# Short key tile as one strip, and the last peaks, count, constants and value copies moved behind the pieces

## The reference, cut to what matters

```python
q = x @ Wq
xc = jnp.concatenate((mem, x), axis=1)          # 154 + 1024 = 1178 keys
k, v = jnp.split(xc @ Wkv, 2, axis=-1)
dots = jnp.einsum('bhid,bhjd->bhij', q, k) * scale
mask = j_idx > i_idx + mem_len
attn = jax.nn.softmax(jnp.where(mask[None, None], -jnp.inf, dots), axis=-1)
out = jnp.einsum('bhij,bhjd->bhid', attn, v)
x = x + (out @ Wout + bout)                     # x enters attention layer-normalised
x = x + ffn(layernorm(x))                       # top-k routing, 8 experts
```

## Time and profile before

| | us |
|---|---|
| median of 3 runs | 374.89 (374.08 to 375.56) |
| the profiled execution, its own time | 374.39 |
| its span, first to last instruction | 372.3 |
| PE busy | 350.2 (94%) |
| ACT busy | 265.4 (71%) |
| DVE busy | 209.0 (56%) |
| POOL busy | 117.1 (31%) |
| mean granted TensorE clock | 0.977 of 2.4 GHz |

### The profile page before, as it was taken

How to read it: one execution, slowest core, us unless ns; L and a number is a source line. 1 busy time by engine, 2 the same in 40 slices (tenths; PEclk the granted TensorE clock), 3 DMA queues, 4 the chain that set the end, 5 groups by cost and what they waited for, 6 DMA issues and landing times.

```text
span 372.3 us, 10987 instructions
## 1 busy us (share of the span) xinstructions
PE 350.2 (94%) x4336; PEld 227.7 (61%) x4336; DVE 209.0 (56%) x724; ACT 265.4 (71%) x385; POOL 117.1 (31%) x178
## 2 busy tenths in 40 slices
PE   8999999899999999999999999995858899999993
PEld 7757547353545444453535444584747899999992
DVE  4999788453636546463545546598788232323231
ACT  2675564999999999999999999515861545454530
POOL 5445677000000303012030303602422655555422
PEclk9999999999999999999999999999696999999998
DMA  7724798600548535562549513700660422322200
GB/s 251 192 91 130 241 251 295 209 11 3 143 122 260 126 101 138 166 162 66 126 129 267 130 38 87 243 0 2 229 225 11 139 87 73 98 81 85 61 24 31
DMA packets 37325, 47.68 MB, mean 128 GB/s; under 512 B 8764, under 2 KB 26610, under 8 KB 37265
## 3 DMA queue, kind: packets, MB, share of 16 engines
q1 hardware_dynamic: 34368, 40.26, 37.0%
q0 software_dynamic: 2560, 6.30, 5.6%
q10 hardware_dynamic: 337, 0.32, 0.3%
HBM read 32.71 MB, written 13.81 MB: 125 GB/s over the span
## 4 chain that ended last, share of the span: by engine, by line
PE 79%; ACT 9%; DVE 7%; issue 2%; POOL 2%; POOLq 0%
PE ps L1121 19%; PE ps L1097 18%; PE ps L1302 10%; PE ps L1314 9%; PE ps L1082 8%; ACT pbuf L863 8%; PE ps L1034 5%; PE ps L1004 2%; PE ps L1235 2%; DVE stats L1671 1%; DVE xe L1666 1%; PE ps L1291 1%; PE ps L1183 1%; POOL pbuf L759 1%; PE ps L1018 1%
## 5 line engine op out<-in xcount | busy, mean ns | idle before, releaser
L863 ACT ACTIVATE pbuf<-ps 128x1024 f32<-128x1024 f32 (+3 forms) x192 | 168.6, 1035 | 0.4 <-PE ps L1097 0.4
L1637 DVE SCALAR_TENSOR_TENSOR pbuf<-pbuf,seen 128x128 f32<-128x128 f32 (+2 forms) x288 | 74.0, 294 | 64.2 <-ACT pbuf L863 63.5
L1097 PE MATMUL ps<-q_st,k_st 98*32 98x512 bf16 (+4 forms) x2048 | 101.4, 318 | 2.8 <-ACT pbuf L863 2.6
L1121 PE MATMUL ps<-pbuf,v_st 128*32 128x512 f32 (+4 forms) x1024 | 96.8, 473 | 0.1
L1097 PEld LDWEIGHTS ps<-q_st,k_st 98*32 98x32 bf16 x2048 | 51.8, 96 | 68.3 <-issue 25.6
L729 POOL TENSOR_TENSOR mid<-mid 64x256 f32<-64x256 f32 x28 | 20.2, 751 | 74.7 <-DVE pbuf L1637 63.4
L1121 PEld LDWEIGHTS ps<-pbuf,v_st 128*32 128x32 f32 x1024 | 27.2, 109 | 24.7 <-issue 11.8
L1302 PEld LDWEIGHTS ps<-mid,piece_f 128*128 128x128 f32 x320 | 38.7, 192 | 1.6 <-issue 0.7
L1302 PE MATMUL ps<-mid,piece_f 128*128 128x128 f32 x320 | 39.0, 275 | 0.5 <-issue 0.5
L1314 PE MATMUL ps<-pbuf,mid 128*128 128x256 f32 x160 | 37.7, 379 | 0.0
L945 ACT ACTIVATE mid<-ps 128x512 f32<-128x512 f32 x20 | 11.9, 597 | 34.4 <-PE ps L1302 34.3
(11 more groups left out here) (253 smaller groups left out, 382.6 us busy)
## 6 DMA issues: line engine op xcount, KB each, us to landing
wts<-in_L_ffn_W SPq DMA_DIRECT2D x16, 512.0 KB, 5.1
k_st<-k_cut SPq DMA_DIRECT2D x48, 147.2 KB, 2.9
q_st<-q_cut SPq DMA_DIRECT2D x48, 128.0 KB, 2.9
q_cut<-wts SPq DMA_DIRECT2D x8, 384.0 KB, 3.6
k_cut<-wts SPq DMA_DIRECT2D x8, 384.0 KB, 3.7
token_rows<-xe SPq DMA_DIRECT2D x4, 512.0 KB, 4.2
mid<-mid SPq DMA_DIRECT2D x28, 64.0 KB, 2.5
mid<-reciprocals SPq DMA_DIRECT2D x28, 64.0 KB, 2.3
```

The source lines that it names most:

```text
L863: nc.scalar.activation(pbuf[:, s % 2, r, c0:c1], st_ps[(s * GH + r) % NST][:, c0:c1], ACT.Exp, scale=SCALE).then_inc(exp_done, 1)
L1097: last = nc.tensor.matmul(st_ps[(s * GH + r) % NST][c:c + 32, a:z], k_st[pa][:, r, t * P + c:t * P + c + 32], q_st[pa][:, r, q0 + a - c0:q ...
L1121: last = nc.tensor.matmul(o_ps[32 * r:32 * r + 32, a:z], v_st[pa][:, t, r, :], pbuf[:, s % 2, r, a + dc:z + dc], start=(t == 0), stop=(t = ...
L1637: last = nc.vector.scalar_tensor_tensor(a, a, 3.0e38, seen[:, off:off + w], ALU.min, ALU.mult)
```

## The change

- **Tile 9 as one strip.** Its keys for head r now stand in partitions 32r to 32r + 25 of one tile. In the value jobs ("v", b, 8) tile 9 becomes, per half of the contraction and head, one matmul of 32 rows by 64 columns into the strip of that head. In the scores, heads 0 to 2 drop tile 9; with head 3, four matmuls (one per head) fill the four strips. The exponentials of heads 0 to 2 end 26 columns earlier, one mask (with the new constant `seen_short`) serves four heads, and the values of all four heads take tile 9 from head 3's probabilities, against a `v_st` that is zero outside the head's strip. GpSimd's `load_v` makes four copies of 32 partitions and one of the other nine tiles.
- **Last peaks and count.** ("n", 1) and ("o", 1) leave the loop over jobs; their matmuls follow the scores of step 1, head 0 and head 1, of the first group. `count_over(1)` and `set_flag(1)` open VectorE's `masks(0)`. v(1, 8) now follows v(1, 6), and the flag is read ahead of it. The wait for the banks is split up among the first three scores.
- **Extra matmuls.** Twice four matmuls of 128 columns whose result is not used, in the first step of the first group (`keep_first`).
- **VectorE.** `order_constants` moves from piece 16 to behind `bound(1)`, with four small copies more; of the last three bias additions one follows there, two stand ahead of the masks of steps 4 and 5 of the first group.
- **GpSimd.** The first two `load_v` move from ahead of piece 15 to behind the last piece.

```diff
+SHORT = JT - 1
+SHORT_KEYS = J - SHORT * P
...
-                   k1[1][2], v1[1], ("m", 1), v1[2], v1[3], ("n", 1), v1[4], ("o", 1)])
+                   k1[1][2], v1[1], ("m", 1), v1[2], v1[3], v1[4], ("n", 1), ("o", 1)])
...
             def load_v(pa, b, m):
+                for r in range(GH):
+                    nc.gpsimd.tensor_copy(v_st[pa][32 * r:32 * r + 32, SHORT, r, 0:HD],
+                                          v_all[32 * r:32 * r + 32, b, SHORT, (g * GH + r) * HD:(g * GH + r + 1) * HD]).then_inc(short_in, 1)
+                    pool.wait_ge(short_in, (b * NG + g) * GH + r + 1)
...
-                if i == PER_B + 5:
-                    pool.wait_ge(vcopy_done, len(VJ) // 2)
-                    for pa in range(2):
-                        load_v(pa, 0, 0)
...
+            pool.wait_ge(low_done, len(QK))
+            pool.wait_ge(vcopy_done, len(VJ) // 2)
+            for pa in range(2):
+                load_v(pa, 0, 0)
...
+                        end = c1 - SHORT_KEYS if STEPS[s][-1][0] == SHORT and r < GH - 1 else c1
...
-            for jn, job in enumerate(JOBS):
+            for jn, job in enumerate(JOBS[:-2]):
                 b, bk = job[1], job_bank(jn)
-                if jn == len(JOBS) - 1:
+                if jn == len(JOBS) - 3:
                     fl = shifted(0)
...
+                            for r in range(GH):
+                                mine = bk[32 * r:32 * r + 32, i * D:(i + 1) * D].rearrange("p (g h c) -> p g h c", g=NG, h=GH)
+                                w_ap = wkv_sb[:, k, D:2 * D].rearrange("p (g h c) -> p g h c", g=NG, h=GH)
+                                last = nc.tensor.matmul(mine[:, :, r, :], xcT[:, b, k, SHORT * P:SHORT * P + 32], w_ap[:, :, r, :],
+                                                        start=(k == 0), stop=(k == KT - 1), skip_group_check=True)
...
+                    if t == SHORT:
+                        for h in range(GH if r == GH - 1 else 0):
+                            last = nc.tensor.matmul(st_ps[(s * GH + r) % NST][32 * h:32 * h + 32, c0:c0 + SHORT_KEYS],
+                                                    k_st[pa][:, h, t * P:t * P + 32], q_st[pa][:, h, q0:S],
+                                                    start=True, stop=True, skip_group_check=True)
+                        continue
...
-                                                pbuf[:, s % 2, r, a + dc:z + dc],
+                                                pbuf[:, s % 2, GH - 1 if t == SHORT else r, a + dc:z + dc],
...
+            def last_peaks():
+
+                bk = job_bank(len(JOBS) - 2)
+                pe.wait_ge(bound_done, 2 * KT * 2)
+                nc.tensor.matmul(bk[:, 0:2 * KT], heads[:, :], bpeak[:, 1, :, :].rearrange("p m c -> p (m c)"),
+                                 start=True, stop=True).then_inc(proj_ready, 1)
+
+            def last_count():
+
+                free_bank(len(JOBS) - 1 - NBK)
+                bk = job_bank(len(JOBS) - 1)
+                pe.wait_ge(over_done, 2)
+                nc.tensor.matmul(bk[0:1, 0:1], over[:, 1:2], ones_b[:, 0:1], start=True, stop=True).then_inc(proj_ready, 1)
+
+            def keep_first(n):
+
+                free_bank(len(JOBS) - 2 - NBK)
+                for _ in range(n):
+                    nc.tensor.matmul(o_ps[:, 0:P], ones_b[:, :], ones_b[:, :], start=True, stop=True)
...
                         scores(pa, s, r, g0)
+                        if g0 == 0 and (s, r) == (0, NST - 1):
+                            keep_first(4)
+                        if g0 == 0 and (s, r) == (1, 0):
+                            last_peaks()
+                        if g0 == 0 and (s, r) == (1, 1):
+                            last_count()
                     values_before(0, pa, s, g0, before_g)
                     scores(pa, s, NST, g0)
+                    if g0 == 0 and s == 0:
+                        keep_first(4)
...
-                elif i == 16:
-                    order_constants()
...
             bound(1)
-            count_over(1)
-            set_flag(1)
-            for n in range(5, TT // 2):
-                add_bias(n)
+            order_constants()
+            add_bias(5)
...
             def masks(g0):
 
+                if g0 == 0:
+                    count_over(1)
+                    set_flag(1)
                 for s in range(1, NSTEP):
+                    if g0 == 0 and s >= NSTEP - 2:
+                        add_bias(TT // 2 + s - NSTEP)
...
+                            if t == SHORT:
+                                if r == GH - 1:
+                                    a = pbuf[:, s % 2, r, c0:c0 + SHORT_KEYS]
+                                    last = nc.vector.scalar_tensor_tensor(a, a, 3.0e38, seen_short[:, 0:SHORT_KEYS], ALU.min, ALU.mult)
+                                continue
```

More of the change, by code:

```diff
@@ L109 @@
 LAST = NB * NG - 1
+SHORT = JT - 1
+SHORT_KEYS = J - SHORT * P
+assert SHORT_KEYS <= 32 and GH == 4 and any(len(tiles) > 1 and tiles[-1] == SHORT for tiles in STEP_TILES)
 NARROW = STEP_TILES.index([1])
@@ L211, in xattn_ffn @@
         seen = sb("seen", [P, P])
+        seen_short = sb("seen_short", [P, 32])
         irow = sb("irow", [P, 1], I32)
@@ L284, in xattn_ffn @@
         v_in = sem("v_in")
+        short_in = sem("short_in")
         biased = sem("biased")
@@ L690, in _ @@
             for i in range(2):
-                nc.gpsimd.memset(v_st[i][0:J - (JT - 1) * P, JT - 1, :, HD:HD + 1], 1.0).then_inc(st_made, 1)
-                made += 1
+                for r in range(GH):
+                    nc.gpsimd.memset(v_st[i][32 * r:32 * r + SHORT_KEYS, SHORT, r, HD:HD + 1], 1.0).then_inc(st_made, 1)
+                    made += 1
             pool.wait_ge(st_made, made)
@@ L862, in exps @@
                             act.wait_ge(pv_done, g0 * NSTEP + s + 1)
-                        nc.scalar.activation(pbuf[:, s % 2, r, c0:c1], st_ps[(s * GH + r) % NST][:, c0:c1], ACT.Exp,
+                        nc.scalar.activation(pbuf[:, s % 2, r, c0:end], st_ps[(s * GH + r) % NST][:, c0:end], ACT.Exp,
                                              scale=SCALE).then_inc(exp_done, 1)
@@ L1033, in _ @@
                         for k in range(KT):
-                            last = nc.tensor.matmul(bk[:, i * D:(i + 1) * D], xcT[:, b, k, (t + i) * P:(t + i + 1) * P],
-                                                    wkv_sb[:, k, D:2 * D], start=(k == 0), stop=(k == KT - 1))
+                            if t + i < SHORT:
+                                last = nc.tensor.matmul(bk[:, i * D:(i + 1) * D], xcT[:, b, k, (t + i) * P:(t + i + 1) * P],
+                                                        wkv_sb[:, k, D:2 * D], start=(k == 0), stop=(k == KT - 1))
+                                continue
+                            for r in range(GH):
+                                mine = bk[32 * r:32 * r + 32, i * D:(i + 1) * D].rearrange("p (g h c) -> p g h c", g=NG, h=GH)
+                                w_ap = wkv_sb[:, k, D:2 * D].rearrange("p (g h c) -> p g h c", g=NG, h=GH)
+                                last = nc.tensor.matmul(mine[:, :, r, :], xcT[:, b, k, SHORT * P:SHORT * P + 32], w_ap[:, :, r, :],
+                                                        start=(k == 0), stop=(k == KT - 1), skip_group_check=True)
                 elif job[0] == "s":
@@ L1084, in _ @@
                 last.then_inc(proj_ready, 1)
-            for jn in range(len(JOBS) - NBK, len(JOBS) - 2):
+            assert JOBS[-2:] == [("n", 1), ("o", 1)]
+            for jn in range(len(JOBS) - NBK, len(JOBS) - NBK + 2):
                 free_bank(jn)
@@ L1168, in group @@
                     for r in range(NST):
+                        if g0 == 0 and s == 0 and r > 0:
+                            for jn in range(len(JOBS) - NBK + 2 * r, len(JOBS) - NBK + 2 * r + 2):
+                                free_bank(jn)
                         scores(pa, s, r, g0)
+                        if g0 == 0 and (s, r) == (0, NST - 1):
[4 more added lines that the diff above has]
+                            last_count()
                     values_before(0, pa, s, g0, before_g)
                     scores(pa, s, NST, g0)
+                    if g0 == 0 and s == 0:
+                        keep_first(4)
                     values_before(1, pa, s, g0, before_g)
@@ L1467, in order_constants @@
                 seq(nc.vector.tensor_scalar(seen[:, :], fcol[:, :], frow[:, 0:1], None, ALU.is_ge))
+                for r in range(GH):
+                    seq(nc.vector.tensor_copy(seen_short[32 * r:32 * r + 32, :], seen[0:32, 0:32]))
             def digit_constants():
@@ L1656, in _ @@
             seq(nc.vector.memset(mx, -3.0e38))
-            v.wait_ge(flag_done, 2)
             for g in range(2 * NG):
                 if g % (2 * KT) == 0:
+                    v.wait_ge(flag_done, g // (2 * KT) + 1)
                     fl = v.value_load(flag[0:1, g // (2 * KT):g // (2 * KT) + 1], min_val=0, max_val=1)
```

8 lines of the change are left out of this document (5 added, 3 removed).

## The result

| | before | after |
|---|---|---|
| median of 6 runs each | 374.57 us (374.08 to 375.56) | 372.32 us (372.12 to 372.75) |
| ratio, 95% interval | | 0.9939 [0.9924, 0.9954] |
| the profiled execution, its span | 374.39, 372.3 | 372.7, 370.8 |

The account below looks back on a forecast made before the run. TensorE was taken to bound the head, ScalarE and TensorE both full in attention. From 374.39, minus 1.94 (head) and 0.10 (attention) gives 372.35; the median's 0.50 more gives 372.85, predicted 372.8 us; 8-in-10 range 372.0 to 374.2.

Parts of the forecast that it names:

- Strips of a value job: Value jobs ("v", b, 8) in the head: tile 9 as strips saves 0.63 us per job, 1.18 instead of 1.82.
- rival 2: Value jobs: the strips bring nothing, the moving operand being read in runs of 16 elements; gain 0.78, 374.1 us; chance 0.12.
- First exponential 1.94 us earlier: End of the head: scores start at 63.99, 1.98 us earlier, and the first exponential at 64.70 instead of 66.64.
- then scores can follow: TensorE behind the last value job: its strip rounds end at 64.62 and scores follow; 1.35 us before 65.97, 0.63 from strips.
- What stood before the scores in the kernel before: TensorE's queue ahead of the scores at 65.97: the count's matmul at 65.56, the flag's read (0.89) and the branch (0.37).
- (a) The late piece: Scores wait for GpSimd's last piece, needed by about 63.3, expected at 62.8 to 63.3; no loss, up to 0.9 as bound.
- rival 1: Head: VectorE and GpSimd contend, the last piece is late, scores start at 64.85; gain 1.06 + 0.1, 373.7 us; chance 0.19.
- VectorE and GpSimd hinder each other: Both engines behind the pieces: contention stretches a bias addition from 0.68 to 1.49 us, the moved work from about 5 to 6.5.
- Attention 0.1 us: Eight attention groups: shorter step 3 exponentials save 0.06 per group, shrunk to about 0.01 because step 4 waits for TensorE.
- rival 3: Attention: the shorter exponentials pay in full, 0.5 us for 0.1, giving 372.4 us; chance 0.09.
- Rival 4, the clock: Start of attention: TensorE's clock falls to 1.2 GHz between sparse scores, costing 3.4 us, giving 376.2 us; chance 0.05.
- The extra matmuls' drains: Four places between scores: eight tiling-mode steps, 0.7 us, lie in TensorE's slack of 0.47 us per exponential; cost 0.

## Why the prediction was right, and where it was not

- **Strips of a value job**, predicted 1.18 us start to next start: 1.20. The way there (strips by the L1052 row) holds, and rival 2 is out: short runs of the moving operand cost nothing.
- **First exponential 1.94 us earlier**: 1.68, from ("v", 0, 8) on. By the strip jobs the sum was right (25.96 against 26.82 to the last value job, of which 0.22 are the peaks). What was missed is the step "then scores can follow": 0.54 us from the first strip to the first score, where 0.23 was put. So the mis-sized term is the time between the last job and the scores, 0.3 us. The waits and the branch in TensorE's queue are taken only as the strips begin, and 0.21 of the 0.3 came back when they were moved ahead.
- **What stood before the scores in the kernel before** was put down to the count's matmul and the read with its branch. Right, but the read was dismissed too easily: "with v(1, 6) and v(1, 8) to cover it" was the clause that mattered. With strips in the last job and peaks, count and read left in place, the head is 1.9 us longer than after.
- **(a) The late piece**, rival 1: the last subtraction was expected 0 to 0.5 us ahead of the point where it decides; it had 1.8 us to spare (25.18 + 0.51 against 27.45). With the constants or the copies in their old place it decides indeed, and that costs 1.2 and 0.7 us. So rival 1 describes what the change avoids. The moved work on VectorE and GpSimd was costed at nothing, and does cost nothing: peaks at 66.60, count at 67.72, first values at 68.33, predicted 67.2, 68.1 and 69 (the early start alone takes 0.9 off each).
- **VectorE and GpSimd hinder each other**: yes, but "the moved work grows from about 5 to 6.5 us" took it for a rate. The runs show a lock: the mask's four copies took 0.79 or 1.77 us, the block of constants 3.2 or 4.8, by which of GpSimd's instructions they met. The Trainium skill (Trainium Architecture — The Big Picture, What this means for kernel authors) calls the ports that the two share an exclusive lock and not a split of bandwidth; the traces agree, with ends 0.03, 0.08 and 0.55 us behind GpSimd's.
- **Attention 0.1 us** failed: it was 0.54, rival 3's size, though not by its reason. The step that failed is "so the 0.06 per group shrink to about 0.01": it took the start of step 4's first exponential for the moment from which ScalarE's time counts. In the kernel after the start is indeed held up nearly as long as I said; but exponentials overlap, and a start some 60 ns late doesn't move an end. 26 columns cost 22 ns three times a group, all on the path.
- **Rival 4, the clock**: 1.00 in the kernel after. It fell where it wasn't looked for, in an execution of the kernel before. So the argument against this rival, that the first scores were as sparse before at full clock, held for one execution and not for all; a fall cost 1.5 us, not 3.4.
- **The extra matmuls' drains** lie in TensorE's slack as was said: the head and the pitch are the same without them (28.13 and 21.00 us). The Trainium skill (TensorEngine Tiling (Array Packing), Key Properties) says that a change of tiling mode drains TensorE. With the row's 0.09 us a step, the estimate was 0.7 us; no run here shows it as lost time.
- **The sum**: 1.94 + 0.10 = 2.04 predicted, 1.68 + 0.54 = 2.22 measured, 2.25 between the medians. The two errors, 0.26 too much and 0.44 too little, nearly cancel, and that is luck. So is a part of the match with the medians: the sum put everything behind the last exponential and outside the span at no change, and these were -0.5 and +0.2.

## What to carry to other kernels

Parts of a change need not add up: here one part alone is slower than before, because it made two small blocks dearer in a place where VectorE and GpSimd share, and took away the matmuls that had covered a slow read in TensorE's queue. When a job gets shorter, ask what it was covering. And on an engine whose instructions overlap, read the spacing of ends, not of starts, before a saving is written off.

## What the runs showed of the hardware

- ScalarE's exponentials from PSUM overlap: durations of 1000 to 1130 ns at ends 916 ns apart (1024 columns, fp32).
- TensorE's waits, reads and branches behind sixteen strip matmuls and their weight loads are taken only as these start (62.89 in the kernel after), behind wide matmuls 3.6 us ahead (the read at 58.3, its job at 61.9); a read of a flag takes 0.3 to 1.2 us of the queue.
- VectorE's additions, multiplications, comparisons and copies that read SBUF alone and meet an instruction of GpSimd end a fixed time behind it (128x512 addition 0.55 us, 128x128 0.08, 32x32 copy 0.03), whenever they began; GpSimd's 128x512 subtraction that meets such an addition under way ends 1.01 to 1.03 us behind it. Reductions of 128x512 (0.67 us) and operations with one operand in PSUM (0.68) are not stretched.
- GpSimd's copies of 32 x 16 elements in a chain take 0.24 us each, a third of one of 128 x 576 (0.66), and 0.35 beside VectorE's work (0.94 to 0.97 and 1.42 for four).
- Executions of one kernel differ by when the clock reaches 2.4 GHz at the start (("v", 0, 8) at 35.66 to 37.03 us) and, in some, by a fall to 1.2 GHz in the first group of attention (1.5 us).
